# A two-layer gated cross-attention block on one core: the last feed-forward stage over tokens sorted by expert

## The reference

```python
x = hidden_states.reshape(-1, 256)                  # 2048 tokens
expert_idx = jnp.argmax(x @ W_router, axis=-1)      # one of 4 experts for each token
h = gelu(jnp.einsum('th,ehi->tei', x, W1) + b1)     # W1: 4 x 256 x 1024
intermediate = h of the token's own expert          # onehot sum over e
y = intermediate @ Wo + bo + x                      # Wo: 1024 x 256, shared
y = layer_norm(y, gamma, beta)
x_out = x_in + tanh(g_ffn[1]) * y
```

## Time and profile before

| what | us |
|---|---|
| median of 3 runs (lowest, highest) | 936.2 (930.4, 936.54) |
| the profiled execution's own time | 929.45 |
| its span in the profile | 927.6 |
| outside of the span | 1.85 |
| granted TensorE clock over the span | 0.946 of full speed |

### The profile page before, as it was taken

One profiled execution on the slowest core, in us unless ns is written; L12 is line 12 of the kernel. 1 busy time (PEld: TensorE's weight loads), 2 busy tenths in 40 slices (PEclk: granted clock), 3 DMA queues, 4 the chain that ended last, 5 costly groups with the idle time before them and its releaser, 6 DMA issues. The chain is left out here.

```text
span 927.6 us, 11844 instructions
## 1 busy us (share of the span) xinstructions
PE 830.7 (90%) x4356; PEld 493.6 (53%) x4356; DVE 578.5 (62%) x932; ACT 438.6 (47%) x821; POOL 249.8 (27%) x277
## 2 busy tenths in 40 slices
PE   6885999999989889975999999964999999999984
PEld 3442344343337678752443334323778778778764
DVE  4573899999516936576898999738815136036026
ACT  2222788888855376502788878873210210210110
POOL 2130555455532286501000000115211120120220
PEclk9996999999999999987899999995999999998998
DMA  7695222222032300263145322020000000000000
GB/s 269 173 218 163 64 74 74 71 70 71 2 104 81 89 1 0 71 160 91 52 119 169 120 72 71 3 63 1 2 0 1 1 23 1 1 23 1 0 24 23
DMA packets 40539, 60.67 MB, mean 65 GB/s; under 512 B 7257, under 2 KB 17241, under 8 KB 40481
## 3 DMA queue, kind: packets, MB, share of 16 engines
q1 hardware_dynamic: 37216, 55.84, 21.2%
q0 software_dynamic: 864, 0.92, 1.3%
q10 hardware_dynamic: 2400, 3.15, 1.0%
HBM read 40.02 MB, written 18.87 MB: 63 GB/s over the span
## 5 line engine op out<-in xcount | busy, mean ns | idle before, releaser
L1118 DVE TENSOR_REDUCE row_max<-ps_wide 128x2 f32<-128x1024 f32 x256 | 301.2, 1220 | 31.5 <-PE ps_wide L479 25.1
L829 ACT ACTIVATE probs<-ps_a 128x512 f32<-128x512 f32 x342 | 191.5, 602 | 42.4 <-PE ps_a L535 37.3
L479 PE MATMUL ps_wide<-stack_k,stack_q 48*128 48x512 f32 x512 | 154.3, 470 | 15.8 <-DVE row_max L1118 11.3
L535 PE MATMUL ps_a<-stack_q,stack_k 62*128 62x512 f32 (+1 forms) x342 | 139.4, 456 | 11.8 <-ACT probs L829 11.4
L549 PE MATMUL ps_out<-probs,vals 128*17 128x512 f32 x1024 | 135.6, 604 | 0.5 <-POOL probs L978 0.5
L932 ACT ACTIVATE hid_full<-ps_a 128x512 f32<-128x512 f32 x32 | 19.1, 598 | 216.1 <-PE ps_a L748 154.5
L535 PEld LDWEIGHTS ps_a<-stack_q,stack_k 62*128 62x128 f32 (+1 forms) x342 | 60.8, 190 | 99.5 <-ACT probs L829 71.9
L829 ACT ACTIVATE probs<-ps_misc 128x512 f32<-128x512 f32 x170 | 102.4, 603 | 18.0 <-PE ps_misc L535 13.8
L978 POOL TENSOR_TENSOR probs<-probs,fixes_sb 128x512 f32<-128x512 f32 x64 | 81.9, 1280 | 82.7 <-ACT probs L829 82.7
L1037 POOL TENSOR_TENSOR hid_lo<-hid_full,hid_hi 128x512 fp32r<-128x512 f32 x32 | 42.5, 1331 | 192.8 <-ACT hid_hi L933 192.8
L479 PEld LDWEIGHTS ps_wide<-stack_k,stack_q 48*128 48x128 f32 x512 | 62.3, 190 | 52.5 <-DVE row_max L1118 21.0
(11 more groups left out here) (166 smaller groups left out, 1236.2 us busy)
## 6 DMA issues: line engine op xcount, KB each, us to landing
planes_k<-planes SPq DMA_DIRECT2D x32, 256.0 KB, 3.8
planes_q<-planes SPq DMA_DIRECT2D x32, 256.0 KB, 3.8
stack_q<-planes_q SPq DMA_DIRECT2D x64, 128.0 KB, 2.8
stack_k<-planes_k SPq DMA_DIRECT2D x64, 128.0 KB, 2.8
stack_q<-planes_q SPq DMA_DIRECT2D x64, 64.0 KB, 2.7
stack_k<-planes_k SPq DMA_DIRECT2D x64, 64.0 KB, 2.6
w_e_raw<-in_L_W SPq DMA_DIRECT2D x4, 1024.0 KB, 5.4
w_raw<-in_L_W SPq DMA_DIRECT2D x2, 1024.0 KB, 6.2
```

The source lines that it names most:

```text
L479: mm(raw_slot(("pair", g, p))[:, i * S:(i + 1) * S], stack_q[at, slot(g, c) + q * P:slot(g, c) + (q + 1) * P], stack_k[at, slot(g, c):slot ...
L535: mm(score_slot(("tile", n))[:], stack_k[at, slot(g, c) + k * P:slot(g, c) + (k + 1) * P], stack_q[at, slot(g, c):slot(g, c) + S], start=T ...
L829: do(probs[n % PROBS][:, j, :], score_slot(("tile", n * HG + j))[:], ACT.Exp, scale=0.25).then_inc(exp_done, 1)
L1118: v.tensor_reduce(row_max[:, g % 2, :, p], raw_slot(("pair", g, p))[:].rearrange("p (i k) -> p i k", i=2), AX, ALU.max).then_inc(sem(f"max ...
```

## The change

**What is computed.** Each token goes through its own expert only. Tokens are sorted into blocks of 128 that belong to one expert. Rounding each expert up to whole blocks gives at most 16 + 3 = 19 blocks (`BLOCKS`). They run in two phases: the first 5 (`FIRST`) are whole blocks filled from rows 0 and 1, the other 14 (`SECOND`) come from all four rows.

**How tokens are sorted.** For a row, VectorE's `route` makes the one-hot matrix and a running count for each expert; TensorE's `count` makes each token's place by matmuls with a triangle of ones; `place` turns it into an address; GpSimd scatters the token numbers into a table in DRAM with 4 indirect DMAs (`place_ids`). `tables(phase)` (some 18 small VectorE instructions) finds which expert and which table row each block has. GpSimd fetches the table rows (`fetch_ids`), TensorE turns them (`turn_ids`), VectorE keeps them (`keep_ids`), and then each block's rows (normed and plain `x`, 2 KB for each token, written to DRAM by SyncE's `keep_rows`) are gathered with one indirect DMA (`gather`). The result goes back by an indirect scatter (`scatter`).

**Where it stands.** `turn_n3`, `route_logits`, `count`, `route` and `place` of rows 0 and 1 are put into groups 14 and 15 of attention 1 on TensorE, VectorE and ScalarE. The expert weights are split by GpSimd alone, three pieces of 512 columns after each group's maxima from group 6 on, `Wo` at group 13 and the bias at group 6 (with a wait of SyncE for `b1_cleared` between two of its `send_maximum`). Probabilities in attention 1 have 4 buffers instead of 6.

```diff
-            for b in range(B):
-                for f in range(FC):
...
+            def up(n):
+
+                wait(pe, sem("hid1_ready"), 2 * n)
+                pe.wait_ge(sem("offset_ready"), 1 + int(n >= FIRST))
+                at = nc.tensor.value_load(offset[0:1, n:n + 1], min_val=0, max_val=(E - 1) * C * FF)
+                for half in range(2):
+                    bank = pw[0][:, half * S:(half + 1) * S]
                     for i, (r, w) in enumerate(PRODUCTS):
...
+                        for c in range(C):
+                            mm(bank, sortedT[r][:, n % 2, c, :], w1_flat[w][:, bass.ds(at + (c * FF + half * S), S)],
+                               start=(i == 0 and c == 0), stop=False)
+                    mm(bank, select[0:HOT, n, :], b1_parts[0:HOT, half * S:(half + 1) * S], start=False, stop=True
                        ).then_inc(sem("up1_done"), 1)
...
+            for n in range(BLOCKS):
+                if n == FIRST:
+                    pe.wait_ge(sem("selected"), 2)
+                up(n)
+                if n + 1 < BLOCKS and n != FIRST - 1:
+                    turn_rows(n + 1)
+                if n == 0:
+                    turn_n3(3)
+                if n == 1:
+                    route_logits(3)
+                if n > 0:
+                    down(n - 1)
+                turn_hidden(n)
+                if n == 1:
+                    count(3)
+                    total(1)
+                if n == FIRST - 2:
+                    turn_ids(1)
+                if n == FIRST - 1:
+                    turn_rows(n + 1)
+            down(BLOCKS - 1)
```

ScalarE, GpSimd and VectorE in the last stage:

```diff
+            rows_high(0)
+            for n in range(BLOCKS):
+                for half in range(2):
+                    act.wait_ge(sem("up1_done"), 2 * n + half + 1)
...
+                    do(hid1[:, n % 2, half * S:(half + 1) * S], pw[0][:, half * S:(half + 1) * S], ACT.Gelu
+                       ).then_inc(sem("hid1_ready"), 1)
+                if n + 1 < BLOCKS and n != FIRST - 1:
+                    rows_high(n + 1)
...
+                for half in range(2):
+                    act.wait_ge(sem("hid1_turned"), 2 * n + half + 1)
...
+                    do(hid1T[0][:, n % 2, half * FC // 2:(half + 1) * FC // 2], ps[half][:].rearrange("p (f t) -> p f t", t=P), ACT.Copy
...
+            for n in range(2, BLOCKS + 2):
+                if n < BLOCKS:
+                    root4(n)
+                scatter(n - 2)
+                m = n + ROW_RING - 2
+                if FIRST + 3 <= m < BLOCKS:
+                    gather(m)
...
+                if n >= ROW_RING:
+                    pool.wait_ge(sem(f"stored_{n % LANDING}"), 16 * ((n - ROW_RING) // LANDING + 1))
...
+            for n in range(BLOCKS + 2):
+                if n == FIRST - 1:
+                    keep_ids(1)
+                if n + 1 < BLOCKS and n != FIRST - 1:
+                    rows_low(n + 1)
+                if 0 < n <= BLOCKS:
+                    residual(n - 1)
+                if n < BLOCKS:
+                    hidden_low(n)
+                if n == 1:
+                    route(3)
+                if n == 2:
+                    place(3)
+                    tables(1)
+                if n == 3:
+                    finish(0)
+                if n > 2:
+                    finish(n - 2)
+                if 0 < n <= BLOCKS:
+                    spread(n - 1)
```

GpSimd in attention 1, and SyncE at group 6:

```diff
+                    if l == 1 and g == G - 3:
+                        hidden_weights()
                     if g + BEHIND < G:
                         split_maximum(l, g + BEHIND)
...
+                    if l == 1 and g >= WEIGHTS_FROM:
+                        for n in range(3 * (g - WEIGHTS_FROM), min(3 * (g - WEIGHTS_FROM) + 3, E * QT)):
+                            expert_weights(*divmod(n, QT))
+                    if l == 1 and g == WEIGHTS_FROM:
+                        split_bias()
...
+                    if l == 1 and g == 2 + E:
+                        load_last()
```

More of the change, by code:

```diff
@@ new lines, in turn_hidden, with down @@
+            def turn_hidden(n):
+                for half in range(2):
+                    pe.wait_ge(sem("hid1_ready"), 2 * n + half + 1)
+                    wait(pe, sem("hid1_low"), 2 * n - 1 + half)
+                    for f in range(FC // 2):
+                        at_f = (half * FC // 2 + f) * P
+                        last = tr(ps[half][:, f * P:(f + 1) * P], hid1[:, n % 2, at_f:at_f + P], ident[:])
+                    last.then_inc(sem("hid1_turned"), 1)
+            def down(n):
+                wait(pe, sem("down1_read"), n)
@@ L756, in _ @@
[L756 to L764 removed]
+                        last = mm(po[:, 0:D], hid1T[r][:, n % 2, f, :], w_mo_part(w, f),
+                                  start=(f == 0 and i == 0), stop=(f == FC - 1 and i == 2))
@@ L1375, in _, with keep_ids @@
-            for q in range(QT + 1):
-                if q < QT:
-                    residual((B - 1) * QT + q)
-                    variance4(B - 1, q)
-                if q > 0:
-                    finish(B - 1, q - 1)
+            def keep_ids(phase):
+                i, j = slots(phase)
+                dve.wait_ge(sem("ids_turned"), phase + 1)
+                v.tensor_copy(ids[:, i:j], ids_bank(phase)[:, 0:j - i]).then_inc(sem("ids_ready"), 1)
+            route(2)
+            keep_ids(0)
```

759 lines of the change are left out of this document (485 added, 274 removed).

## The result

The changed kernel takes 874.5 us (median of 4 runs, 871.4 to 877.65), the kernel before on the same chip 935.41 (930.4 to 936.54). The ratio is 0.936, its 95% interval 0.931 to 0.941: faster, as forecast and inside the range of 808 to 880, but 42 us above the 832 that I gave. The profiled execution took 877.65 us, the longest of the four, with a span of 875.9; the sum of the prediction was 829, so 49 us have to be found.

What follows compares the result with a forecast made beforehand. TensorE, busy 90% of the span, was taken as the bound. First block at 646, plus 156 for 19 blocks, 6, 5, 14 and 1.85 outside the span gave 829 us; adjusted to 832, range 808 to 880.

Steps and rivals of the forecast that it cites:

- rival (b): Last stage: GpSimd sets the pace, with 2.5 us per indirect DMA and 4 to land; 868 us, chance 0.18.
- Together 7.35 us of TensorE: Last stage, one block: up 3.40 (14 matmuls at 0.243), down 2.89 and ten transposes 1.05 us.
- I take 0.85: Register load ahead of each last-stage block: 0.85 us, between bounds of 0 and 4.0, making 8.2 us a block.
- rival (a): Last stage: the register load is hidden wholly, 19 x 0.85 = 16 us less; 816 us, chance 0.18.
- next, 2 us behind: Last-stage blocks: TensorE sets the pace at 8.2 us; VectorE follows with 6.1 us of work.
- Rival (c): Last stage: VectorE sets the pace, its 6.1 us a block becoming 8.8; 843 us, chance 0.10.
- fetch 1, landing 3: Second phase's ids: after four scatters and their landing, fetch 1 us, landing 3; chain 13.6 us, TensorE waits 5.
- is off it: Before the first block: GpSimd's chain for the ids, done at 637, does not delay the start at 646.
- 10 us go into attention: End of attention 1: routing rows 0 and 1 there moves the last values from 619.4 to 629.5 us.
- +3 us (0 to 6): Attention 1, group 6: SyncE's loads and wait for b1_cleared take 14 us against 11, adding 3 us.
- rival (e): Last stage: TensorE's clock stays low because every block has new waits; 970 us, chance 0.03.
- block 5: Last stage, after the second phase's ids: block 5's gather (1 + 3 us) fits beside block 4.

Runs made afterwards that it cites:

- the mends: Changed kernel with ids 32 bytes apart, last loads, bias split and blank ids later, block 5's rows split first, unread matmuls in waits: ratio 0.900.

## Why the prediction was right or wrong

The 49 us are these (the forecast's figures first; 603.9 was its last regular turned output). Attention is 6 us later there: 609.87. From it to up(0): 42.1 against 58.2, +16. From up(0) to the last matmul at 859.5: 169 (156, 6.3, 5 and the 1.9 ahead of the last down) against 191, +22; all of it lies ahead of block 5's turn_hidden, where 83.3 us stand against 58.8. From the last matmul to the end: 13.6 against 18.2, +5, half of it the landing of the last scatter, 5.4 us to the end of the span where I had 3.

The measured 874.5 lies nearest to rival (b)'s 868, and that is chance: (b)'s mechanism, 2.5 us for the issue of an indirect DMA and GpSimd's loop as the pace of the blocks, did not come. Slow landings did, but only those of the ids. That the time fell inside the range owes something to it, since the upper end was (b)'s.

- *"Together 7.35 us of TensorE", the block's sum*: mis-sized. The bias matmul was counted as one of 14 at 0.243 us; by its 36 rows it costs 0.4 us a half more (2.01 for 1.61). The 0.243 was a mean over 24 matmuls and one bias matmul, and I took it over to a place with one in seven, though the chain had the 0.43 by itself. With 128 rows the pitch is 7.15, 0.2 under my sum.
- *"I take 0.85", the register load*: wrong; rival (a) for this term. With a fixed address the pitch stays at 7.93. The two errors nearly cancelled, by luck: 7.93 measured, 8.2 forecast.
- *VectorE "next, 2 us behind", GpSimd's loop "below 8.2"*: right, with 6.1 of 8.2 us forecast and 0.69 of the time measured for VectorE (5.5 of 7.93). Rival (c) did not come. An indirect DMA's issue is 0.93 to 1.13 us.
- *"fetch 1, landing 3" behind "four scatters 4.0, landing 3"*: the step that failed for the ids. Their scatters land in 7.1 to 17 us, since they write 4 bytes beside 4 bytes. In phase two TensorE waited 10 us where I had 5. That the ids chain of phase one *"is off it"* failed with it: the fetch went out 17.2 us behind the last scatter where I had 3, TensorE waited 8.4 us for it, and up(0) came 16 us late. Not all of the 16 is the ids: with the ids apart up(0) still came 48.7 us after the last regular turned output, where I had 42.1, since attention ended so late.
- *"10 us go into attention"*: 19 did (38.5 against 19.4 from the last regular to the last turned output). In the profile VectorE waits 6.7 and 4.1 us for TensorE's two counts there, and ScalarE up to 4.6 and 5.6 for scores held up behind them. It made little difference in the end: with all of it after attention the rest is 3.4 us longer before the mends and 0.4 after, neither clear of what two executions differ by. I had taken this part for what lets the blocks begin early.
- *"+3 us (0 to 6)" at group 6*: 5.4, inside the bounds, but not for SyncE's wait for b1_cleared. GpSimd's memset ended at 528.32 and the load behind it began at 528.35, after the seventh load's end at 528.19: 0.2 us of waiting. It was the nine issues ahead of the maxima, 3.0 us late, and their landing in 5.3. The run with the loads moved alone showed that the bias rows' landing stands right behind. The other 3.5 us of shift come from before attention 1, and mostly from the first 85 us, where executions differ.
- *The cold clock*, rival (e), was set against attention's 0.97. It did come, for part of the stage: about 13 us. The rows had a warning, 0.61 in the stretch from 616 to 648, where TensorE waits; the waits ahead of up(0), up(2) and up(4) and inside up(5), 2.1 to 10 us long, were each followed by matmuls at half clock.
- *block 5* was said to fit beside block 4. It did not: VectorE split its rows behind finish and spread, and TensorE waited 3.4 us for them; with the split put ahead that wait is gone, so it was the order of the code, not the DMA.
- *"nothing is added" by the weight splits*: right. Groups 9 to 14 of the changed kernel come 11.0 to 12.0 us apart, like before.
- *"some 2 us less in all"*, the aside on four landings, comes to nearer 3 by its own figures (four times 3 us against four times 2.0 and the bytes); no other number uses it.

With the clock, the ids, the stall and block 5 mended, up(0) to block 5's turn_hidden takes 58.3 us; my terms gave 58.8 for it (five blocks of 8.2, the extra 6.3 and 5, and 6.5 for block 5's up, rows and down). That they meet is partly luck again: the 58.8 holds register loads and waits that are gone in this run, and lacks the price of the bias matmuls. What was missing in the forecast were waits and the clock behind them.

## What to carry to other kernels

A wait that a change adds to TensorE costs more than its length where the clock falls in it: here about 13 us on top of some 27 us of waits, and matmuls that nobody reads took that back. They must be shorter than the wait, though: where the ids came early, 20 of them held up what they should have bridged. Price the landing of a scatter by how its pieces lie in DRAM, ahead of their number; neighbouring 4-byte writes were the longest wait on the path here, and giving each 32 bytes of its own mended it. And look for matmuls of few rows between full ones: with zeros up to 128 rows they were cheaper here. A mean over many equal matmuls and one odd one hides the odd one's price, and a change can make it more frequent.

## What the runs showed of the hardware that I had not expected

- A scatter of 128 ids of 4 bytes side by side landed 7.6 us after the end of its issue alone, four 7.1 to 8.7, eight 14.6 to 17.2 over the kernels; at a distance of 32 bytes four or eight had landed 1.5 us after the last issue, and 1.9 us in one of the kernels. Why eight take so much longer than four was not tried, nor were distances other than 4 and 32 bytes.
- A bias matmul of 36 rows cost 0.4 us more than one of 128 in the middle of matmuls of 128 rows.
- With the bias at 128 rows the clock rose from half to full some 3 us into an up (663.08 to 666.2), and somewhere inside all 3 ups behind a wait; with 36 rows 18 of 24 ups behind a wait stayed at half for all of their 7.15 us, and 6 did not. Whether the rows of the bias matmul have a part in this, or only the moment at which the up begins, was not separated.
- Loading a block's weight offset into a register on TensorE did not show in the pitch: 7.93 us with it and without.
